# Gated graph layer: the products of a zero matrix between the block sums are taken out

## The chip, the cores and the metric

One core of one Trainium2 chip runs the whole program. A core has five engines that run beside each other and wait for one another by semaphores: TensorE (PE, matmuls; PEld is its loading of the stationary operand), VectorE (DVE), ScalarE (ACT), GpSimd (POOL) and SyncE (SP, which only issues DMAs here). The metric is the device time of one execution in microseconds (us), lower is better; a measured time is the median of several runs. [...]

## The reference, cut to what matters

The program is two graph layers and two expert layers over 3,125 nodes with 256 features and 100,000 edges. The change lies in the third part, the gated graph layer:

```python
def _L1_gnn_ref(x, src, dst, W_w, W_b, U_w, U_b, V_w, V_b, attn_l, attn_r, gamma, beta):
    Wh = x @ W_w + W_b
    Uh = x @ U_w + U_b
    Vh = x @ V_w + V_b
    out_src = Wh * attn_l
    out_dst = Wh * attn_r
    sigma = jax.nn.sigmoid(out_src[src] + out_dst[dst])
    sum_sigma_h = jax.ops.segment_sum(Vh[src] * sigma, dst, num_segments=N)
    sum_sigma = jax.ops.segment_sum(sigma, dst, num_segments=N)
    h = Uh + sum_sigma_h / (sum_sigma + 1e-06)
    mu = jnp.mean(h, axis=-1, keepdims=True)
    var = jnp.mean((h - mu) ** 2, axis=-1, keepdims=True)
    h = (h - mu) / jnp.sqrt(var + 1e-06) * gamma + beta
    h = jax.nn.relu(h)
    return x + h
```

Its result is normalized again and goes through the first linear layer with a GELU and the gate (`gelu(xn @ W1 + b1)`, `@ Wg + bg`) of the last expert layer, which `stage_strips` computes on the way.

## The kernel before, in words

The stages run one after another. `stage_strips` is the gated layer. The nodes lie in 25 blocks of 128 (`NB`), a block in four strips of 32 nodes. A block takes 10 steps (`QC`), so there are 250 steps `g`, with `i = g % 10`. In steps i = 0 to 7 each strip brings 128 edges of its own (tiles of 128 x 1024: four strips of 256 features); in steps 8 and 9 there is one group of 128 mixed edges (128 x 256).

A step passes through the engines like this; the names in quotes are those of the tiles, without the stage's prefix `strips_`:

- POOL (L2461) gathers the rows of the edges' source nodes, one indirect DMA for each strip: 4 in steps 0 to 7, 1 in step 8, 33 for a block (and a single one for all the tenth steps). They land in a ring of 12 slots (`RING`; eight slots are parts of `Wd`, four are `G`). A slot is asked for again once the gate product of its last user is done (`s_use`). The last block has only two strips with edges of their own, so it has 17 gathers.
- DVE makes the two masks (L2475 `ohT`, L2478 `oh`) two steps ahead.
- PE `expand` (L2627) multiplies the destination nodes' rows by `ohT` into `p_b`: four matmuls of 96 x 256, bf16. It runs two steps ahead too.
- DVE `add` (L2494): `tv` = gathered row + `p_b`. ACT (L2568, L2571): two sigmoids of `tv`, into `p_s` and into half of `sv`. DVE (L2504): gathered row x `p_s` into the other half of `sv`.
- PE `sums` (L2639): `sv` is added into the block's 32-node strips of `p_sg`, four f32 matmuls side by side in the array (eight records in the trace).

Between the steps of a block stand the pieces of the three blocks ahead of it (`tail(b, i)`): layer norms on DVE; on PE the transposes of the normalized block (L2661, with step i = 4), the linear layer (L2672) in groups of 6, 6 and 4 products of f32 (12, 12 and 8 records) with steps i = 5, 6 and 7, the gate (L2681, L2686) and the transposes of the hidden rows (L2688 with i = 2, L2693 with i = 4); on ACT the copy `xT` of the transposed block (L2590, i = 4), the GELU (L2599, i = 9). Every engine runs its list strictly in that written order. So ACT cannot start the sigmoids of the step after i = 4 before `xT` is copied, and `xT` needs PE's `sums` of step i = 4 and the transposes behind it.

On PE the list of one step is: `expand(g + 2)`; in the steps i = 1 to 4 four products of the zero tile `nil` (128 x 128 by 128 x 512, bf16) that are added to the block's sum `p_sg`; `sums(g)`; and the tails. The zero products (L2650) wait for nothing but the buffer's one memset (L2553).

Of the kernel before, what the change touches and what calls it, by code (L numbers as in the profile page):

```python
# [15 lines left out]
BF16 = mybir.dt.bfloat16  # L16
# [7 lines left out]
P = 128  # L24
N = 3125
D = 256
# [11 lines left out]
H = 4  # L38
# [40 lines left out]
QC = QR + QM  # L79
QB = -(-N // 32)  # L80
NG4 = NB * QC
RR = 4
RING = 12
QP = 32
# [54 lines left out]
def alloc(nc, ctx, stage=""):  # L139

    def sb(name, shape, dt=F32):
        return ctx.enter_context(nc.sbuf_tensor(stage + name, shape, dt))

    def ps(name, shape, dt=F32):
        return ctx.enter_context(nc.psum_tensor(stage + name, shape, dt))

    sems = []

    def clear():

        if sems:
            nc.clear_and_free_semaphores(sems)  # L152
            for s in sems:
                nc.release_semaphore(nc.alloc_semaphore(s.name + "_back", s.num))

    ctx.callback(clear)

    def sem(name):
        sems.append(nc.alloc_semaphore(stage + name))
        return sems[-1]  # L160

    return sb, ps, sem
# [2146 lines left out]
def stage_strips(nc, C, A):  # L2309


    with ExitStack() as ctx:
        sb, ps, sem = alloc(nc, ctx, "strips_")
        G = [C.Wd[:, k * FC * D:(k + 1) * FC * D].rearrange("p (h d) -> p h d", h=H) for k in range(NE)] + [sb(f"G{k}", [P, H, 2 * D]) for k in range(NE, RING)]
        row = [sb(f"row{k}", [ST, H, P], BF16) for k in range(RR)]; ipt = sb("ipt", [ST, P]); ip = sb("ip", [ST, 1])
        oh = [sb(f"oh{k}", [P, H, QP]) for k in range(4)]; nil = sb("nil", [P, 2 * D], BF16)
        ohT = [sb(f"ohT{k}", [ST, H * P], BF16) for k in range(2)]
        tv = [sb(f"tv{k}", [P, H, D]) for k in range(2)]; wrs = [sb(f"wrs{k}", [ST, H, D], BF16) for k in range(3)]
        sv = [sb(f"sv{k}", [P, H, 2 * D]) for k in range(2)]
# [6 lines left out]
        p_sg = [ps(f"p_sg{k}", [P, 2 * D]) for k in range(2)]; p_h = ps("p_h", [P, F])  # L2326
        s_g = [sem(f"s_g{k}") for k in range(RING)]
        Gs = sb("Gs", [P, 1, 2 * D]); s_gs = sem("s_gs")
        s_row = [sem(f"s_row{k}") for k in range(RR)]; s_ip = sem("s_ip"); s_wr = [sem(f"s_wr{k}") for k in range(3)]; s_oT = sem("s_oT"); s_nil = sem("s_nil"); s_oh = sem("s_oh"); s_b = sem("s_b"); s_t = sem("s_t")
        s_s = sem("s_s"); s_s2 = sem("s_s2"); s_use = sem("s_use"); s_sg = sem("s_sg"); s_tot = sem("s_tot")  # L2330
        s_u = [sem(f"s_u{k}") for k in range(2)]; s_w = sem("s_w"); s_wg = sem("s_wg"); s_l4 = sem("s_l4"); s_lt = sem("s_lt"); s_d = sem("s_d"); s_ur = sem("s_ur"); s_var = sem("s_var"); s_std = sem("s_std")
        s_q = sem("s_q"); s_var2 = sem("s_var2"); s_std2 = sem("s_std2"); s_n = sem("s_n"); s_xn = sem("s_xn"); s_tr = sem("s_tr"); s_hr = sem("s_hr"); s_hd = sem("s_hd"); s_xd = sem("s_xd"); s_Wd = sem("s_Wd")
# [57 lines left out]
        with nc.Block(no_gpsimd_drain=True) as block:  # L2390
# [77 lines left out]
            def _(v):  # L2468
                with when_even(C, v, 1):
                    def masks(g):  # L2470
                        b, i = divmod(g, QC)
                        v.wait_ge(s_row[g % RR], 16 * (g // RR + 1))
                        if g >= 2:
                            v.wait_ge(s_b, g - 1)
                        nc.vector.tensor_scalar(ohT[g % 2][:, :], row[g % RR][:, :, :].rearrange("p j e -> p (j e)"), ip[:, 0:1], None, ALU.is_equal).then_inc(s_oT, 1)  # L2475
                        if g >= 4:
                            v.wait_ge(s_sg, g - 3)
                        nc.vector.tensor_tensor(oh[g % 4][:, :, :], C.iota[:, 0:QP].unsqueeze(1).broadcast_to([P, H, QP]),  # L2478
                                                C.dlq[:, b * H:(b + 1) * H, i:i + 1].broadcast_to([P, H, QP]), ALU.is_equal).then_inc(s_oh, 1)
# [70 lines left out]
                            v.wait_ge(s_l, b + 1)  # L2550
                            nc.vector.tensor_tensor(C.lg[:, b, :], ffn(b)[:, 512:512 + NE], bg[:, :], ALU.add).then_inc(s_lg, 1)

                    nc.vector.memset(nil[:, :], 0.0).then_inc(s_nil, 1)  # L2553
                    masks(0)
                    masks(1)
                    nc.vector.memset(wgp[:, :, :], 0.0).then_inc(s_wg, 1)
# [60 lines left out]
            def _(pe):  # L2617
                with when_even(C, pe, 1):
                    def expand(g):
                        b = g // QC  # L2620
                        pe.wait_ge(s_oT, g + 1)
                        if g % QC == 0:
                            pe.wait_ge(s_wr[b % 3], 48 * (b // 3 + 1))
                        if g >= 1:
                            pe.wait_ge(s_t, g)
                        for j in range(H):
                            t = nc.tensor.matmul(p_b[:, j % wide(g), :], ohT[g % 2][:, j * P:j * P + P], wrs[b % 3][:, j, :],  # L2627
                                                 start=(j < wide(g)), stop=(wide(g) == H or j == H - 1))
                        t.then_inc(s_b, 1)

                    def sums(g):
                        b, i = divmod(g, QC)
                        pe.wait_ge(s_use, g + 1)
                        pe.wait_ge(s_s, g + 1)
                        pe.wait_ge(s_oh, g + 1)
                        if i == 0 and b >= 2:
                            pe.wait_ge(s_tot, 2 * b - 2)
                        for j in range(H):
                            t = nc.tensor.matmul(p_sg[b % 2][j * QP:(j + 1) * QP, :], oh[g % 4][:, j, :], sv[g % 2][:, j % wide(g), :],  # L2639
                                                 start=(i == 0), stop=(i == QC - 1), tile_position=(0, j * QP))  # L2640
                        t.then_inc(s_sg, 1)

                    def group(g):
                        if g + 2 < NG4:
                            expand(g + 2)
                        if g == 1:
                            pe.wait_ge(s_nil, 1)
                        if 1 <= g % QC < 5:
                            for n in range(4):
                                nc.tensor.matmul(p_sg[g // QC % 2][:, :], nil[:, 0:P], nil[:, :], start=False, stop=False)  # L2650
                        sums(g)

                    def tail(b, i):
# [42 lines left out]
                    expand(0)  # L2696
                    expand(1)
                    each_step(group, tail)


# [672 lines left out]
def build(nc, A, out):  # L3373
# [19 lines left out]
    with ExitStack() as ctx:  # L3393
# [46 lines left out]
        with ExitStack() as second:  # L3440
            sb, ps, sem = alloc(nc, second)
            C.ixq = sb("ixq", [P, QN, QR, 2], I32); C.mixed = sb("mixed", [P, NB + 1, 2], I32); C.dlq = sb("dlq", [P, QN, QC])
            stage_experts(nc, C, A)
            ahead.close()
            stage_gated_in(nc, C, A)
            bias.close()
            C.Wd = ctx.enter_context(nc.sbuf_tensor("Wd", [P, NE * FC * D], F32, side="right"))
            stage_strips(nc, C, A)
# [48 lines left out]
```

## Time and profile before

| | us |
|---|---|
| median of 3 runs | 3048.69 (3047.15 to 3051.67) |
| profiled execution: span from its first to its last instruction | 3050.2 |
| share of the span: PE busy | 2502.4 (82%) |
| DVE busy | 2395.6 (79%) |
| POOL busy | 1359.9 (45%) |
| ACT busy | 1169.5 (38%) |
| first gather of `stage_strips` issued, at | 1783.55 |
| last gather issued, at | 2804.42 |
| last matmul of the stage starts, at | 2865.03 |

The page gives no time of the profiled execution other than its span. Times "at" count from the first instruction of the program. The stage with the change lasts from about 1783 to 2866, some 1083 us of the 3050. A busy share is a mean over stages that have different limits, so what bounds this stage has to be read from its own waits. In a row of the timeline the first number is the start, the second how long the instruction or merged group was busy, and brackets hold the engine's idle time before it with the engine that ended it; "issue" stands for time in which it waited for nothing that the profile shows.

### The profile page before, as it was taken

The page shows a single profiled execution, that of the slowest core. Times are in us where ns is not written, and L with a number is a line of the kernel's source. Part 1 is how long each engine was busy: PE and PEld are TensorE (multiplying, and loading weights), DVE is VectorE, ACT ScalarE, POOL GpSimd, SP SyncE. Part 2 cuts the span into 40 slices and gives each one's busy share as a digit, 9 for nine tenths or more (in the row PEclk, how much of TensorE's full clock was granted, in tenths as well). Part 3 has the DMA queues.
Part 4 walks back from the last instruction along what each step waited for, and adds up shares of the span by engine and source line. Part 5 has one row for each costly group of instructions (what it writes and reads, how often), then busy time and mean ns, then how long its engine had stood idle before and what let it go on. Part 6 is the DMA issues. An engine that isn't in the chain of part 4 may idle for free. (4 is left out here: it accounts for less than half of the span.)

```text
span 3050.2 us, 49528 instructions
## 1 busy us (share of the span) xinstructions
PE 2502.4 (82%) x17163; PEld 1226.6 (40%) x17164; DVE 2395.6 (79%) x5109; ACT 1169.5 (38%) x2265; POOL 1359.9 (45%) x1627
## 2 busy tenths in 40 slices
PE   6899869999986999985999756777666777667598
PEld 3555544333353333334666421333333333323365
DVE  6999979999968999979343757777777777777477
ACT  5666750000020000002222434666666666666421
POOL 2888850000000000000650777777777777776055
PEclk8999989999998999995999876888888888888799
DMA  3000010000032000003341577888888888887343
GB/s 123 10 10 10 10 38 15 15 15 15 5 42 40 15 26 18 5 19 107 92 124 43 189 239 240 247 258 259 248 256 259 255 259 256 252 258 241 133 148 106
DMA packets 235579, 373.47 MB, mean 122 GB/s; under 512 B 83273, under 2 KB 165390, under 8 KB 233513
## 3 DMA queue, kind: packets, MB, share of 16 engines
q0 software_dynamic: 75536, 238.14, 25.9%
q1 hardware_dynamic: 156569, 128.66, 14.2%
q10 hardware_dynamic: 3200, 3.21, 0.4%
q8 instruction: 147, 2.41, 0.3%
q14 instruction: 127, 1.04, 0.1%
HBM read 324.84 MB, written 50.04 MB: 123 GB/s over the span
## 5 line engine op out<-in xcount | busy, mean ns | idle before, releaser
L1161 PE MATMUL dense_p_o<-dense_W,feat 128*32 128x512 f32 x7200 | 789.7, 594 | 23.4 <-DVE dense_W L1093 23.4
L1093 DVE SCALAR_TENSOR_TENSOR dense_W<-layer_B,steep,cnt 128x512 f32<-128x512 f32 x1200 | 796.7, 744 | 3.2 <-DVE dense_W L1093 1.8
L2461 POOL DMA_INDIRECT Wd<-tab_d,ixq x544 | 520.7, 957 | 171.2 <-issue 167.5
L1161 PEld LDWEIGHTS dense_p_o<-dense_W,feat 128*32 128x32 f32 x7200 | 261.4, 110 | 520.9 <-issue 399.9
L1572 POOL MEMSET edst<- 128x782 int32 x1 | 0.8, 752 | 936.6 <-POOLq L1210 936.6
L2639 PE MATMUL strips_p_sg<-strips_sv,strips_oh 128*32 128x512 f32 x2000 | 317.7, 713 | 92.7 <-DVE strips_sv L2504 92.7
L2627 PE MATMUL strips_p_b<-strips_wrs,strips_ohT 96*128 96x256 bf16 x1000 | 176.5, 306 | 223.2 <-DVE strips_ohT L2475 204.6
L729 POOL TENSOR_SCALAR mix_L<-mix_back,encode_lowT 128x128 bf16<-128x128 f32 x520 | 320.5, 634 | 55.6 <-PE mix_p_c L889 54.8
L2568 ACT ACTIVATE strips_p_s<-strips_tv 128x1024 f32<-128x1024 f32 (+1 forms) x250 | 225.2, 901 | 163.9 <-DVE strips_sv L2504 149.7
L1117 ACT COPY dense_part<-dense_p_o 128x512 f32<-128x512 f32 x36 | 18.8, 594 | 645.5 <-PE dense_p_o L1161 645.5
L2461 POOL DMA_INDIRECT strips_G<-tab_d,ixq x240 | 229.7, 957 | 73.2 <-issue 71.3
L2494 DVE TENSOR_TENSOR strips_tv<-Wd,strips_p_b 128x1024 f32<-128x1024 f32 (+1 forms) x152 | 175.6, 1155 | 99.8 <-DMA Wd<-tab_d,ixq 61.2
L2627 PEld LDWEIGHTS strips_p_b<-strips_wrs,strips_ohT 96*128 96x128 bf16 x1000 | 94.0, 106 | 360.3 <-DVE strips_ohT L2475 317.2
L2571 ACT ACTIVATE strips_sv<-strips_tv 128x1024 f32<-128x1024 f32 (+1 forms) x250 | 228.6, 914 | 0.1
L2504 DVE TENSOR_TENSOR strips_sv<-Wd,strips_p_s 128x1024 f32<-128x1024 f32 (+1 forms) x152 | 174.7, 1149 | 63.4 <-ACT strips_p_s L2568 63.2
L738 DVE TENSOR_SCALAR mix_R<-encode_ramp,encode_keyT 128x250 bf16<-128x250 uint16 (+2 forms) x784 | 183.1, 299 | 0.0
L746 DVE TENSOR_TENSOR cnt<-cnt,mix_p_c 128x500 f32 x196 | 130.7, 667 | 23.9 <-PE mix_p_c L889 21.6
L889 PE MATMUL mix_p_c<-mix_R,mix_L 128*128 128x250 bf16 (+2 forms) x784 | 128.7, 291 | 14.9 <-DVE cnt L746 12.6
L2650 PE MATMUL strips_p_sg<-strips_nil 128*128 128x512 bf16 x400 | 136.3, 475 | 0.0
L2672 PEld LDWEIGHTS strips_p_h<-strips_xT,strips_w 128*128 128x128 f32 x768 | 104.7, 216 | 65.2 <-issue 65.2
L2639 PEld LDWEIGHTS strips_p_sg<-strips_sv,strips_oh 128*32 128x32 f32 x2000 | 42.1, 115 | 189.4 <-DVE strips_sv L2504 139.4
L2672 PE MATMUL strips_p_h<-strips_xT,strips_w 128*128 128x128 f32 x768 | 118.1, 309 | 0.0
(540 smaller groups left out, 3883.2 us busy)
## 6 DMA issues: line engine op xcount, KB each, us to landing
strips_row<-dlr_d SPq DMA_DIRECT2D x250, 96.0 KB
ew<-in_ew SPq DMA_DIRECT2D x16, 1024.0 KB, 5.4
layer_B<-rise_d SPq DMA_DIRECT2D x12, 1024.0 KB, 4.8
hx_d<-hrow SPq DMA_DIRECT2D x24, 512.0 KB, 2.8
Wd<-tab_d,ixq POOLq DMA_INDIRECT x544
Wd<-in_fWd SPq DMA_DIRECT2D x8, 1024.0 KB, 9.0
tab_d<-feat SPq DMA_DIRECT2D x50, 128.0 KB, 2.5
tab_d<-gated_in_rowg SPq DMA_DIRECT2D x25, 256.0 KB, 2.0
```

What stands on the lines that cost most here:

```text
L729: nc.gpsimd.tensor_scalar(L[g % NL][:, j, :], back[:, :], lowT[:, i, j * CP + p:j * CP + p + 1], None, ALU.is_equal).then_inc(s_Lp, 1)
L738: nc.vector.tensor_scalar(own(g, j), near_keys(j), keyT[:, i, j * CP + p:j * CP + p + 1], None, ALU.is_equal).then_inc(s_oh, 1)
L1093: o = nc.vector.scalar_tensor_tensor(out=out, in0=rise, scalar=C.steep[:, q * H + h:q * H + h + 1], in1=count, op0=ALU.max, op1=ALU.mult)
L1161: m = nc.tensor.matmul(p_o[c % 2][h * MT:(h + 1) * MT, a, 0:n], feat[:, q, h, lo:lo + MT], W[t % 3][:, h, 0:n], start=(q == 0), stop=(q == ...
L2461: gp.indirect_dma_start(out=G[n % RING][:, j, :], out_offset=None, in_=C.tab3[:, :], in_offset=bass.IndirectOffsetOnAxis(ap=index, axis=0) ...
L2494: nc.vector.tensor_tensor(tv[g % 2][:, 0:wide(g), :], rows(g)[:, :, 0:D], p_b[:, 0:wide(g), :], ALU.add).then_inc(s_t, 1)
L2504: nc.vector.tensor_tensor(sv[g % 2][:, 0:wide(g), 0:D], rows(g)[:, :, D:2 * D], p_s[:, 0:wide(g), :], ALU.mult).then_inc(s_use, 1)
L2568: nc.scalar.activation(p_s[:, 0:wide(g), :], tv[g % 2][:, 0:wide(g), :], ACT.Sigmoid).then_inc(s_s2, 1)
L2571: nc.scalar.activation(sv[g % 2][:, 0:wide(g), D:2 * D], tv[g % 2][:, 0:wide(g), :], ACT.Sigmoid).then_inc(s_s, 1)
L2627: t = nc.tensor.matmul(p_b[:, j % wide(g), :], ohT[g % 2][:, j * P:j * P + P], wrs[b % 3][:, j, :], start=(j < wide(g)), stop=(wide(g) == ...
L2639: t = nc.tensor.matmul(p_sg[b % 2][j * QP:(j + 1) * QP, :], oh[g % 4][:, j, :], sv[g % 2][:, j % wide(g), :], start=(i == 0), stop=(i == Q ...
L2672: t = nc.tensor.matmul(ffn(b)[:, q * P:q * P + P], w1[:, kc, q * P:q * P + P], xT[:, kc * P:kc * P + P], start=(kc == 0), stop=(kc == KC - 1))
```

## The change

The four zero products are taken out of the steps i = 1 to 4 of each block, with the tile `nil`, its memset on DVE, its semaphore and PE's one wait for it. They are 4 x 4 x 25 = 400 matmuls and as many weight loads. What they added to the sums was zero.

```diff
-        oh = [sb(f"oh{k}", [P, H, QP]) for k in range(4)]; nil = sb("nil", [P, 2 * D], BF16)
+        oh = [sb(f"oh{k}", [P, H, QP]) for k in range(4)]
...
-                    nc.vector.memset(nil[:, :], 0.0).then_inc(s_nil, 1)
                     masks(0)
                     masks(1)
...
                     def group(g):
                         if g + 2 < NG4:
                             expand(g + 2)
-                        if g == 1:
-                            pe.wait_ge(s_nil, 1)
-                        if 1 <= g % QC < 5:
-                            for n in range(4):
-                                nc.tensor.matmul(p_sg[g // QC % 2][:, :], nil[:, 0:P], nil[:, :], start=False, stop=False)
                         sums(g)
```

No other instruction changes its place on any engine. PE's list at a step i = 4 of a block and at i = 5 behind it, before (`strips_p_b` is `expand`, `strips_nil` the zero tile, `strips_p_sg<-strips_sv` the sums, `strips_p_h` the transposes and the linear layer):

```order
L2627 MATMUL strips_p_b<-strips_wrs,strips_ohT 128x256 x4
L2650 MATMUL strips_p_sg<-strips_nil 128x512 x4
L2639 MATMUL strips_p_sg<-strips_sv,strips_oh 32x512 x4
L2693 MATMUL strips_p_h<-ident,strips_HT 128x128 x4
L2661 MATMUL strips_p_h<-ident,strips_xn 128x128 x2
L2627 MATMUL strips_p_b<-strips_wrs,strips_ohT 128x256 x4
L2639 MATMUL strips_p_sg<-strips_sv,strips_oh 32x512 x4
L2672 MATMUL strips_p_h<-strips_xT,strips_w 128x128 x6
```

and the same place on PE in the changed kernel, where the line numbers are smaller by 1 to 6:

```order
L2626 MATMUL strips_p_b<-strips_wrs,strips_ohT 128x256 x4
L2638 MATMUL strips_p_sg<-strips_sv,strips_oh 32x512 x4
L2687 MATMUL strips_p_h<-ident,strips_HT 128x128 x4
L2655 MATMUL strips_p_h<-ident,strips_xn 128x128 x2
L2626 MATMUL strips_p_b<-strips_wrs,strips_ohT 128x256 x4
L2638 MATMUL strips_p_sg<-strips_sv,strips_oh 32x512 x4
L2666 MATMUL strips_p_h<-strips_xT,strips_w 128x128 x6
```

The row of the zero products is gone and nothing has moved past anything else.

## Rows read from the trace of the kernel before

**Rows 1.** The page: busy time of the engines; POOL and granted clock in 40 slices.

```profile
PE 2502.4 (82%) x17163; PEld 1226.6 (40%) x17164; DVE 2395.6 (79%) x5109; ACT 1169.5 (38%) x2265; POOL 1359.9 (45%) x1627
...
POOL 2888850000000000000650777777777777776055
PEclk8999989999998999995999876888888888888799
```

**Rows 2.** Stretches of the stage: blocks 1 to 22, last block, its tail.

```profile
core 0: us, PE busy (x) PEld busy (x) DVE busy (x) ACT busy (x) POOL busy (x), PEclk, DMA share, GB/s
...
1833.00:2753.60 920.60, 659.62 (x4243) 290.40 (x4246) 683.92 (x1233) 581.42 (x857) 698.37 (x730) 0.85 0.84 254
...
2798.00:2839.00 41.00, 30.94 (x196) 13.97 (x199) 30.68 (x55) 26.48 (x40) 5.70 (x6) 0.83 0.82 265
2839.00:2866.00 27.00, 18.62 (x162) 14.70 (x159) 6.96 (x20) 15.67 (x43) 0.00 (x0) 0.81 0.21 72
```

**Rows 3.** Timeline of POOL: the first gather, two in block 23, the last.

```profile
1783.55 0.98 POOL L2461 DMA_INDIRECT Wd<-tab_d,ixq  x1 [5.66 <-issue]
...
2757.70 0.95 POOL L2461 DMA_INDIRECT Wd<-tab_d,ixq  x1 [0.30 <-issue]
2758.96 0.95 POOL L2461 DMA_INDIRECT Wd<-tab_d,ixq  x1 [0.30 <-issue]
...
2804.42 0.94 POOL L2461 DMA_INDIRECT strips_G<-tab_d,mixed  x1 [0.30 <-issue]
```

**Rows 4.** Waits from 1833 to 2753.6: total us, times, longest us.

```profile
DVE strips_tv L2494 <- DMA Wd<-tab_d,ixq: 34.9, 27, 2.7
DVE strips_tv L2494 <- PE strips_p_b L2627: 26.3, 24, 2.1
DVE strips_tv L2494 <- DMA strips_G<-tab_d,ixq: 20.7, 15, 2.7
...
POOL Wd L2461 <- DVE strips_sv L2504: 3.4, 11, 0.3
```

**Rows 5.** Timeline of DVE: a product in block 22, steps 229, 230, 240, 249.

```profile
2718.02 1.22 DVE L2504 TENSOR_TENSOR strips_sv<-Wd,strips_p_s 128x1024 f32<-128x1024 f32 x1 [0.72 <-ACT strips_p_s L2568]
...
2751.11 0.42 DVE L2494 TENSOR_TENSOR strips_tv<-strips_Gs,strips_p_b 128x256 f32<-128x256 f32 x1 [0.96 <-PE strips_p_b L2627]
...
2753.64 1.22 DVE L2494 TENSOR_TENSOR strips_tv<-Wd,strips_p_b 128x1024 f32<-128x1024 f32 x1 [1.31 <-issue]
...
2798.06 1.22 DVE L2494 TENSOR_TENSOR strips_tv<-Wd,strips_p_b 128x1024 f32<-128x1024 f32 x1 [1.31 <-issue]
...
2836.96 0.42 DVE L2494 TENSOR_TENSOR strips_tv<-strips_Gs,strips_p_b 128x256 f32<-128x256 f32 x1 [0.96 <-issue]
```

**Rows 6.** Timeline of the last block's steps 4 to 6: PE, one DVE product.

```profile
2821.81 1.21 DVE L2504 TENSOR_TENSOR strips_sv<-Wd,strips_p_s 128x1024 f32<-128x1024 f32 x1
...
2822.19 1.29 PE L2650 MATMUL strips_p_sg<-strips_nil 128*128 128x512 bf16 x4
2823.41 1.94 PE L2639 MATMUL strips_p_sg<-strips_sv,strips_oh 128*32 128x512 f32 x8
...
2829.25 1.59 PE L2639 MATMUL strips_p_sg<-strips_sv,strips_oh 128*32 128x512 f32 x8 [2.21 <-DVE strips_sv L2504]
2830.77 2.69 PE L2672 MATMUL strips_p_h<-strips_xT,strips_w 128*128 128x128 f32 x12
...
2833.82 1.06 PE L2639 MATMUL strips_p_sg<-strips_sv,strips_oh 128*32 128x512 f32 x8
2834.82 1.60 PE L2672 MATMUL strips_p_h<-strips_xT,strips_w 128*128 128x128 f32 x12
```

**Rows 7.** What is removed: the zero products' group (page), the memset and first sum.

```profile
L2650 PE MATMUL strips_p_sg<-strips_nil 128*128 128x512 bf16 x400 | 136.3, 475 | 0.0
...
1783.95 0.27 DVE L2553 MEMSET strips_nil<- 128x256 uint32 x1
...
1794.57 1.22 DVE L2494 TENSOR_TENSOR strips_tv<-Wd,strips_p_b 128x1024 f32<-128x1024 f32 x1 [7.63 <-DMA Wd<-tab_d,ixq]
```

More of the change, by code:

```diff
@@ L2328, in stage_strips @@
         Gs = sb("Gs", [P, 1, 2 * D]); s_gs = sem("s_gs")
-        s_row = [sem(f"s_row{k}") for k in range(RR)]; s_ip = sem("s_ip"); s_wr = [sem(f"s_wr{k}") for k in range(3)]; s_oT = sem("s_oT"); s_nil = sem("s_nil"); s_oh = sem("s_oh"); s_b = sem("s_b"); s_t = sem("s_t")
+        s_row = [sem(f"s_row{k}") for k in range(RR)]; s_ip = sem("s_ip"); s_wr = [sem(f"s_wr{k}") for k in range(3)]; s_oT = sem("s_oT"); s_oh = sem("s_oh"); s_b = sem("s_b"); s_t = sem("s_t")
         s_s = sem("s_s"); s_s2 = sem("s_s2"); s_use = sem("s_use"); s_sg = sem("s_sg"); s_tot = sem("s_tot")
```

## The prediction

> **What bounds the kernel now.** I started with the page's busy shares. PE is the busiest engine of the program at 82% [rows 1], which would make every matmul taken out look like a gain. But the change touches one stage only, so I cut that stage into stretches. In the 920.6 us of blocks 1 to 22, PE is busy 659.62 us, DVE 683.92 and ACT 581.42 [rows 2]: none is full. The reader is to see in the same row that POOL has 730 gathers in it, one in 1.26 us. The timeline of POOL says why: two gathers in a row start at 2757.70 and 2758.96, each 0.95 us long with 0.30 us of its own issue before it [rows 3]. That is 1.25 us for a gather however full the other engines are. From 1783.55 to 2804.42 [rows 3] the 810 gathers (24 x 33 + 17 + 1) take 1020.9 us, or 1.26 each. POOL hardly ever stands for a buffer: its waits for DVE's products add up to 3.4 us, the longest 0.3, which is no more than its issue time [rows 4].
>
> The waits confirm it from the other side. DVE's first sum of a step waits for a gather to land 27 + 15 times in that stretch, 34.9 + 20.7 = 55.6 us, 2.5 us for each of the 22 blocks [rows 4]. So the chain of DVE, ACT and PE follows the gathers and catches up with them in most blocks.
>
> How much room lies between the two: the product at 2718.02 ends at 2719.24 and frees the slot of step 220 [rows 5]; twelve slots later that slot is asked for at 2757.70, the first gather of step 233 [rows 3]. The chain could run 38.5 us later before POOL would feel it. But a chain that is late at the end is late by just that amount, ring or no ring, because the last block has half the gathers and is not paced by them: the last gather is issued at 2804.42 [rows 3] and the last sum starts at 2836.96 [rows 5]. What counts is whether the chain keeps up over a block, and how long the last block and its tail take.
>
> The chain's own pace is seen where no gather holds it. In the last block it goes from step 240 at 2798.06 to step 249 at 2836.96, 38.90 us for nine steps; a tenth like the one from 2751.11 to 2753.64 is 2.53, so 41.4 us for a block [rows 5]. Thirty-three gathers at 1.2526 take 41.3 us, and the 22 blocks took 920.6 / 22 = 41.8 each [rows 2]. The two are close. That is the danger in this case: a block is not bound by PE, but a block that gets longer by more than a microsecond or two will be.
>
> **The change, part by part.** *The 400 zero products.* They kept PE busy for 136.3 us [rows 7], 5.5 us a block. In blocks 0 to 23 this is PE time inside a stage that POOL paces, so it is worth nothing as such: the gathers hide it. It can only matter where a zero product runs on past the end of the DVE product that the sums wait for. In step 244 that product ends at 2821.81 + 1.21 = 2823.02 and the sums start at 2823.41, when the zero products are through: 0.39 us late, and behind these sums stand the transposes, ACT's copy and the next sigmoids [rows 6]. In the last block this comes back in full: -0.4 us. In the others it lies behind the gathers: 0. Were the cover gone, it would be -0.4 each, or 24 x -0.4 = -10 us.
>
> *The memset.* DVE loses 0.27 us at 1783.95, and its first sum then waits 7.63 us for the first gather [rows 7]: 0. PE's wait for it never held. The free kilobyte in each partition moves later tiles; no row shows an address to matter, so 0, with nothing to bound it by but the scatter of the runs.
>
> *TensorE's clock.* This is the part with a sign of its own. The granted share in blocks 1 to 22 is 0.85 [rows 2]: PE is at half clock about 30% of the time although the zero products fill its gaps. A row shows what comes before a fall: PE idle 2.21 us for a DVE product, then sums of 1.59 us, where the same sums take 1.06 two steps on [rows 6]. Without the zero products the steps 1 to 4 hold only the expansion and the sums, so PE is idle for most of them, and I expect the half level to spread over these four steps. What it makes of one instruction is in the rows: sums 1.06 to 1.94 us, twelve records of the linear layer 1.60 to 2.69 [rows 6]. In steps 1 to 3 nobody waits for the sums of the same step; the next users come two steps later, so 0.88 us more is hidden. It is not hidden in two places. One is step 4, where the transposes go to ACT; but there the sums are at half clock already in the block shown (1.94), so little is added, and the zero products' delay goes: between -0.4 and, where the sums now run at full, +0.88 - 0.4 = +0.5. The other is steps 5 to 7, where PE has sums and linear layer back to back and is the bound of its steps. In the block shown the first of these groups is slow (1.59 + 2.69 against 1.06 + 1.60, +1.6), the second is fast. If the half level now lasts through the second as well, a block gets 0.88 + 1.09 = 2.0 us longer. That is less than the 2.5 us of waiting for gathers in a mean block [rows 4]. So in blocks 0 to 23 I take 0, with ends of 0 and +2.0 a block. In the last block nothing covers it: between -1.6 (its first group at full) and +2.0; long stretches of work bring the clock back within such a group now, so I take the value near the lower middle, +0.5.
>
> *The tail*, 27 us from 2839 to 2866 at 0.81 [rows 2], starts 17 us after the last zero product at 2822.19 [rows 6]. Its instructions and idle times are the same: 0, ±1.
>
> Sum: -0.4 + 0.5 + 0 = +0.1 on a profiled span of 3050.2. The median of the runs is 3048.69, 1.5 us below that span and inside the scatter of the runs (3047.15 to 3051.67); so 3049 is what I expect to be measured. The likeliest case has its own range of 3045 to 3055: the last block's -2.0 to +2.5, and the scatter.
>
> [...]
>
> **The rivals.** *Slower: the clock makes the chain longer than the gathers.* The place is steps 5 and 6 of a block, the price 2.0 us where the half level reaches the second linear group, and it decides from the point where a block of the chain passes 41.8 us. For it: a free block already takes 41.4 us, so in blocks like that one only 0.4 of the 2.0 is covered, and lateness adds up from block to block. Against it: the mean of 2.5 us of waiting for gathers, and that PE works without a gap from step 4's sums to the transposes, which should lift the clock again before step 5 or soon in it. If half of the blocks pay, 11 x 2.0 + 2 = 24 us: 3073. All of them, with the 0.4 covered: 24 x 1.6 + 2 = 40: 3089.
>
> *Faster: the chain, not POOL, sets the pace, and the zero products' delay in step 4 is on it.* 24 blocks x 0.4 us, and at most the four products' own 1.29 us [rows 6] in each, gives -10 to -31; near the middle, 3029. For it: the closeness of 41.4 to 41.8. Against it: 42 waits for gathers, spread over 22 blocks.
>
> *Faster by all of it: PE is the bound.* 3050.2 - 136.3 = 2914. Only the 82% speaks for it; DVE's waits for PE's `p_b` are 26.3 us in 24 waits [rows 4], and these stand in the steps that have no zero products.
>
> **How the numbers follow.** A measurement of this kernel can tell a change from none at about 0.2%, 6 us. Forecast (no change, 3049): 0.71. Slower by the clock: 0.20. Faster by the delay: 0.08. PE the bound: 0.01. The range has to leave out no more than 0.2: it holds the first case and, of the slower one, the part in which up to a third of the blocks pay (8 x 2.0 + 2 = 18, so to 3067), and on the low side little, since the delay is small: 3042 to 3067. The chances of faster, same and slower are those of the cases: 0.09, 0.71, 0.20.
>
> **What would show it.** In the profile after: POOL's gathers at 1.25 us still, from about 1783.5 to 2804; DVE's waits for landings still there, near 2 us a block; PE's busy time down by less than 136 us in the stage, because what stays runs slower; the granted clock in blocks 1 to 22 down from 0.85 to somewhere between 0.70 and 0.80 (at 0.60 all of steps 1 to 4, four tenths of the time, would have gone from full to half and more); sums at steps 1 to 4 mostly at 1.94 us, at steps 7 to 9 at 1.06. The forecast is wrong if the last gather is issued later than 2810, or if POOL waits for `sv` by more than its own 0.3 us, or if the landings no longer hold DVE: then the chain is the bound and its lateness is the loss.

## The result, and the profile after

| kernel | median, us | range of the runs, us | profiled span, us |
|---|---|---|---|
| before | 3048.57 (10 runs) | 3044.15 to 3057.83 | 3050.2 |
| changed | 3057.15 (10 runs) | 3052.18 to 3061.25 | 3056.2 |

The ratio is 1.0025, with a 95% interval from 1.0016 to 1.0035. The forecast was 3049 us in a range from 3042 to 3067. The time lies in the range, 8 us above the forecast. The prediction took 0.2% (6 us) as the least that can be told from no change; this interval lies on both sides of it, so the loss is clear of zero and hardly more than that. A second measurement, below, gave 1.0012.

The page of the changed kernel, answering to [rows 1] and [rows 7] (busy time, then POOL and the granted clock in 40 slices, then PE's costliest group in this stage):

```profile
span 3056.2 us, 48728 instructions
...
PE 2492.2 (82%) x16763; PEld 1225.9 (40%) x16764; DVE 2393.3 (78%) x5108; ACT 1169.9 (38%) x2265; POOL 1356.0 (44%) x1627
...
POOL 2888850000000000001650767777777777774055
PEclk8999989999998999985999866777777777776799
...
L2638 PE MATMUL strips_p_sg<-strips_sv,strips_oh 128*32 128x512 f32 x2000 | 366.8, 815 | 123.1 <-DVE strips_sv L2504 122.6
```

The zero products' 136.3 us are gone, yet PE is busy only 10.2 us less. The block sums alone take 366.8 us where the same group took 317.7. They run more often at half clock. The granted share has two levels in all 13 profiles, 1.00 (full clock) and 0.50 (half); from 1833 to 2753.6 us it stood at half for 29% of the time before and for 52% in the changed kernel.

The same stretches of the stage as in [rows 2] (blocks 1 to 22, then the last block):

```profile
1833.00:2753.60 920.60, 648.79 (x3875) 286.31 (x3876) 681.09 (x1232) 582.38 (x857) 697.89 (x732) 0.74 0.83 255
```

```profile
2793.00:2835.00 42.00, 31.12 (x176) 13.71 (x176) 30.87 (x55) 26.58 (x40) 5.94 (x7) 0.67 0.83 264
```

The granted clock fell from 0.85 to 0.74, and POOL issued as many gathers in the same time (732 against 730). POOL's first and last gathers, as in [rows 3]:

```profile
1780.83 0.98 POOL L2461 DMA_INDIRECT Wd<-tab_d,ixq  x1 [5.67 <-issue]
```

```profile
2798.57 0.95 POOL L2461 DMA_INDIRECT Wd<-tab_d,ixq  x1 [0.30 <-issue]
2799.82 0.95 POOL L2461 DMA_INDIRECT strips_G<-tab_d,mixed  x1 [0.30 <-issue]
```

The gathers are 1.25 us apart as before, and the 810 of them took 1019.0 us (1020.9 before). DVE's and POOL's waits from 1833 to 2753.6, as in [rows 4]:

```profile
DVE strips_tv L2494 <- PE strips_p_b L2626: 40.4, 19, 3.1
DVE strips_tv L2494 <- DMA Wd<-tab_d,ixq: 10.2, 9, 3.1
DVE strips_tv L2494 <- DMA strips_G<-tab_d,ixq: 9.4, 5, 4.4
...
POOL Wd L2461 <- DVE strips_sv L2504: 5.2, 17, 0.3
```

DVE's waits for landings shrank from 55.6 us to 19.6, that is from 2.5 us a block to 0.9. Its waits for PE grew by 14.1, and its idle time without a visible cause by 16.8 (from 37.9 to 54.7). So the chain is slower, and the cover of the gathers paid for it. The last block has no such cover. DVE's rows from step 240 on, answering to [rows 5], and PE's, answering to [rows 6]:

```profile
2793.20 1.22 DVE L2494 TENSOR_TENSOR strips_tv<-Wd,strips_p_b 128x1024 f32<-128x1024 f32 x1 [1.28 <-issue]
...
2830.01 0.42 DVE L2494 TENSOR_TENSOR strips_tv<-strips_G,strips_p_b 128x256 f32<-128x256 f32 x1 [3.07 <-PE strips_p_b L2626]
...
2833.30 0.42 DVE L2494 TENSOR_TENSOR strips_tv<-strips_Gs,strips_p_b 128x256 f32<-128x256 f32 x1 [1.28 <-issue]
```

```profile
2818.22 1.93 PE L2638 MATMUL strips_p_sg<-strips_sv,strips_oh 128*32 128x512 f32 x8 [0.29 <-DVE strips_sv L2504]
...
2824.27 1.93 PE L2638 MATMUL strips_p_sg<-strips_sv,strips_oh 128*32 128x512 f32 x8 [1.79 <-DVE strips_sv L2504]
2826.13 2.93 PE L2666 MATMUL strips_p_h<-strips_xT,strips_w 128*128 128x128 f32 x12
...
2829.84 1.39 PE L2638 MATMUL strips_p_sg<-strips_sv,strips_oh 128*32 128x512 f32 x8
2831.16 1.60 PE L2666 MATMUL strips_p_h<-strips_xT,strips_w 128*128 128x128 f32 x12
2833.13 1.07 PE L2638 MATMUL strips_p_sg<-strips_sv,strips_oh 128*32 128x512 f32 x8
```

Steps 240 to 249 took 2833.30 - 2793.20 = 40.10 us, 1.2 more than before; 1.0 of it is the wait of step 248 for the expansion, 3.07 us against 2.08. From the first gather to the last product of this stage (`sv`) it is still 1054.2 us against 1055.1. **The stage that was changed lost nothing.** The loss is behind it. From that product to the end of the span, before took 211.6 us and the changed kernel 221.2, although not one instruction differs there. (The stage's start differs by some 7 us between the two profiled executions of the changed kernel, 1780.8 and 1787.4 us, so spans are a poorer guide than such differences.)

That rest consists of the tail, a preparation, and the final stage. The final stage takes 29 tiles. For each POOL gathers `dense_hx`, PE transposes it (`dense_p_t`) and multiplies it by the expert's weights (`dense_p_y`), and POOL scatters `out`. PE at its entrance, first in before, then in the changed kernel (start, length, operation, idle time ahead of it):

```profile
2902.88 1.97 PE L3351 MATMUL dense_p_t<-ident,dense_hx 128*128 128x128 f32 x8 [0.48 <-DMA dense_hx<-hx_d,dense_where]
2905.29 1.10 PE L3351 MATMUL dense_p_t<-ident,dense_hx 128*128 128x128 f32 x8 [0.44 <-DMA dense_hx<-hx_d,dense_where]
2906.32 3.67 PE L3362 MATMUL dense_p_y<-dense_wt,dense_HT 128*64 128x256 f32 x32
```

```profile
2899.82 1.97 PE L3345 MATMUL dense_p_t<-ident,dense_hx 128*128 128x128 f32 x8 [0.27 <-DMA dense_hx<-hx_d,dense_where]
2904.28 1.97 PE L3345 MATMUL dense_p_t<-ident,dense_hx 128*128 128x128 f32 x8 [2.50 <-DMA dense_hx<-hx_d,dense_where]
2906.18 5.07 PE L3356 MATMUL dense_p_y<-dense_wt,dense_HT 128*64 128x256 f32 x32
```

PE waits 2.50 us for the second gather instead of 0.44. The transposes behind it (1.97 against 1.10) and the first products (5.07 against 3.67) then run at half clock (the transposes whole, the products up to 2909.05, where the granted share goes from 0.50 to 1.00). That makes 2.06 + 0.87 + 1.40 = 4.3 us before the first `out` is scattered. What lay beside the gather is seen in DMA traffic cut to a microsecond: "q8 instruction" is an engine's code being fetched, in packets of 16 KB (147 of them make 2.41 MB on the page of before, 16.4 KB each). Before, 2897 to 2898 us, then the changed kernel, 2901 to 2902:

```profile
q8 instruction: 1, 0.02, 5.5%
issues: line engine op xcount, KB each, median us to landing
dense_hx<-hx_d,dense_where POOLq DMA_INDIRECT x1, 4.9
```

```profile
q0 software_dynamic: 62, 0.29, 83.9%
q8 instruction: 1, 0.02, 6.7%
```

In before the packet starts at 2897.1, ahead of the first gather (2897.94), and nothing else moves in that microsecond. In the changed kernel it starts at 2901.0, among 62 packets of the gathers. The second gather, issued at 2896.53, lands after 7.7 us (5.9 before). The profile's page gives the total of that queue: 147 packets before, 144 after. It is PE's code: in blocks 1 to 22 the queue moved 35 packets for 8489 matmuls and weight loads before and 32 for 7751 after, 242 each in both (instructions of PE that only wait are not counted in that). The change takes 400 matmuls and as many weight loads out of PE's list.

How many instructions a packet holds stands in no view; 256 is the author's estimate, and the runs below bear it out. last_only and first_only have 768 instructions of PE fewer than before and three packets fewer (144), 256 to a packet, and their packet starts 0.7 and 0.8 us ahead of the first gather, as in before (0.8). In all_but_last, with 32 fewer, it starts 5.6 us behind that gather, in the changed kernel, with 800 fewer, 5.9. So 768 instructions leave the fetches where they were, and the other 32 of the 800 move them: they fall 32 instructions later in the program. (The total alone would not do as a measure: first_5, with 640 fewer, has 143.)

In the rows at the entrance PE's idle times (0.27 and 2.50 us in the changed kernel) end with a landing of `dense_hx`, not with code. What goes with the packet is seen on POOL's gather.

### The profile page after: what moved, and what is told of

It reads as the page before. It is cut to its first block and busy times, and to the rows that moved or that the text cites. A ratio compares the mean times of both kernels' runs of the same rounds, so it can differ in the third digit from the quotient of the medians.

```text
span 3056.2 us, 48728 instructions
## 1 busy us (share of the span) xinstructions
PE 2492.2 (82%) x16763; PEld 1225.9 (40%) x16764; DVE 2393.3 (78%) x5108; ACT 1169.9 (38%) x2265; POOL 1356.0 (44%) x1627
## 5 line engine op out<-in xcount | busy, mean ns | idle before, releaser
L2638 PE MATMUL strips_p_sg<-strips_sv,strips_oh 128*32 128x512 f32 x2000 | 366.8, 815 | 123.1 <-DVE strips_sv L2504 122.6
L2626 PE MATMUL strips_p_b<-strips_wrs,strips_ohT 96*128 96x256 bf16 x1000 | 201.1, 338 | 202.5 <-DVE strips_ohT L2475 183.8
L729 POOL TENSOR_SCALAR mix_L<-mix_back,encode_lowT 128x128 bf16<-128x128 f32 x520 | 318.9, 630 | 56.5 <-PE mix_p_c L889 55.6
L2626 PEld LDWEIGHTS strips_p_b<-strips_wrs,strips_ohT 96*128 96x128 bf16 x1000 | 105.1, 117 | 373.0 <-DVE strips_ohT L2475 321.2
L2666 PEld LDWEIGHTS strips_p_h<-strips_xT,strips_w 128*128 128x128 f32 x768 | 117.6, 239 | 71.1 <-issue 71.1
L2666 PE MATMUL strips_p_h<-strips_xT,strips_w 128*128 128x128 f32 x768 | 131.8, 334 | 0.0
L2504 DVE TENSOR_TENSOR strips_sv<-strips_G,strips_p_s 128x1024 f32<-128x1024 f32 (+1 forms) x73 | 78.1, 1070 | 47.9 <-ACT strips_p_s L2567 47.9
```

The lines of the kernel that those rows point to most:

```text
L729: nc.gpsimd.tensor_scalar(L[g % NL][:, j, :], back[:, :], lowT[:, i, j * CP + p:j * CP + p + 1], None, ALU.is_equal).then_inc(s_Lp, 1)
L2504: nc.vector.tensor_tensor(sv[g % 2][:, 0:wide(g), 0:D], rows(g)[:, :, D:2 * D], p_s[:, 0:wide(g), :], ALU.mult).then_inc(s_use, 1)
L2666: t = nc.tensor.matmul(ffn(b)[:, q * P:q * P + P], w1[:, kc, q * P:q * P + P], xT[:, kc * P:kc * P + P], start=(kc == 0), stop=(kc == KC - 1))
```

## The experiments

All ratios are to runs of before on the same chip. "Fetches later by", the shift, says by how many instructions the fetches of PE's code fall later in the program than in before: what is missing from PE's list, less whole packets of 256, by the estimate above (400 products are 800 instructions, so 800 - 768 = 32; 192 later is the same as 64 sooner). "2nd gather" is the landing time of the final stage's second `dense_hx` gather. "Rest" is the time from the last `sv` to the end of the span. Both are from the one profiled execution. Medians of different sessions differ by up to 5.6 us for the same kernel, so kernels are compared by the ratio. The last two kernels compute something else (below).

| kernel | zero products kept | fetches later by | median, us | ratio, 95% | 2nd gather, us | rest, us |
|---|---|---|---|---|---|---|
| before | 400 | 0 | 3048.57 | - | 5.9 | 211.6 |
| before_again | 400 | 0 | 3053.54 | 0.9999 (0.9990 to 1.0008) | 6.3 | 211.7 |
| last_only | 16 | 0 | 3052.35 | 0.9992 (0.9983 to 1.0000) | 6.6 | 213.3 |
| first_only | 16 | 0 | 3053.04 | 1.0002 (0.9994 to 1.0011) | 6.3 | 213.2 |
| first_3 | 48 | 192 | 3054.83 | 1.0009 (0.9999 to 1.0020) | 6.3 | 212.9 |
| first_5 | 80 | 128 | 3052.23 | 1.0001 (0.9992 to 1.0010) | 6.0 | 211.1 |
| first_7 | 112 | 64 | 3057.59 | 1.0012 (1.0003 to 1.0021) | 6.2 | 214.5 |
| changed | 0 | 32 | 3057.15 | 1.0025 (1.0016 to 1.0035) | 7.7 | 221.2 |
| after_again | 0 | 32 | 3059.26 | 1.0012 (1.0002 to 1.0023) | 8.3 | 217.7 |
| all_but_last | 384 | 32 | 3056.36 | 1.0010 (0.9998 to 1.0022) | 7.4 | 220.5 |
| all_but_13th | 384 | 32 | 3058.20 | 1.0013 (1.0005 to 1.0022) | 7.6 | 217.4 |
| few_before | 400 | 0 | 3039.67 | 0.9958 (0.9943 to 0.9973) | 5.9 | 216.5 |
| few_after | 0 | 32 | 3046.36 | 0.9972 (0.9961 to 0.9984) | 6.4 | 214.4 |

**The two kernels again.** after_again and before_again are the changed kernel and before, unedited.

> The changed kernel a second time, unchanged. Its first profile has the strips stage no longer than before (first gather to last gate product 1054.2 us against 1055.1), while the stretch from there to the end is 9.6 us longer (221.2 against 211.6), most of it in the final expert stage. Theory A (the chain of DVE, ACT and PE in the strips stage has lost its slack and is late in most executions, just not in the profiled one): this profile shows the stage some 5 to 10 us longer, with the final stage as before. Theory B (the loss is at the end of the strips stage and at the entrance of the final stage, where TensorE comes in at half clock): stage again the same, the end again 5 to 10 us longer. Theory C (the final stage's waits for gathered rows differ from execution to execution and the profiled one was unlucky): end within 3 us of before. All three: ratio to before 1.002 to 1.003.

> The kernel before a second time, unchanged: what the profile of one more execution says of the scatter. Expected by all theories: ratio 1.000 with an interval of 0.1% on either side. Stage from first gather to last gate product 1055 us within 2, the stretch from there to the end 212 us within 3. If that last stretch moves by 5 us or more between two executions of one kernel, the 9.6 us seen between the two first profiles are no evidence for theory B.

The loss came again, at half its first size: 1.0012, below the 1.002 to 1.003 expected. before_again stands at 0.9999. So the true loss is some 0.1 to 0.3%. The changed stage took 1054.3 us, as in the first profile, and the rest of the span is again longer than before's, 217.7 us. before_again's rest is 211.7, as expected; its stage took 1052.7, a little outside the 1055 ± 2 expected. So the stage varies by some 2 us from one execution of a kernel to the next, and the rest of before by 0.1 in these two.

**Zero products in the last block alone, and in all but the last.**

```diff
-                        if 1 <= g % QC < 5:
+                        if 1 <= g % QC < 5 and g // QC == NB - 1:   # last_only
+                        if 1 <= g % QC < 5 and g // QC < NB - 1:    # all_but_last
```

> The zero products only in the last of the 25 blocks (16 of 400). Theory A (loss in the paced blocks 0 to 23): as slow as the changed kernel, ratio 1.002 to 1.003. Theory B (loss in the last block and at the entrance of the final stage): back to the time of before, ratio 1.000. Granted clock of the stage near 0.74 by both.

> The zero products in all blocks but the last (384 of 400). Theory A: time of before, ratio 1.000. Theory B: as slow as the changed kernel, 1.002 to 1.003. Granted clock of blocks 1 to 22 at 0.85 by both.

last_only did as well as before, and all_but_last came out at 1.0010, which is no certain loss by itself. Taken alone that looks as if the last block's zero products were worth 3 us. But all_but_last's stage, first gather to last `sv`, took 1053.1 us, between the 1055.1 and 1052.7 of the two profiles of before. Its rest took 220.5. So the last block had not lost the time, and the same split had two readings: which block keeps them, or how long PE's list is.

**The same two shifts with the last block the other way round.** Both readings are set against each other.

```diff
-                        if 1 <= g % QC < 5:
+                        if 1 <= g % QC < 5 and g // QC == 0:    # first_only
+                        if 1 <= g % QC < 5 and g // QC != 12:   # all_but_13th
```

> The zero products only in block 0 (16 of 400). The traces so far fall into two kinds: where the last block had its zero products and the list of PE is shorter by 0 or 768 instructions (before, last_only), a code fetch of 16 KB lies just before the first gather of the final stage and the second gather lands 5.9 to 6.6 us after its issue; where the last block had none and the list is shorter by 32 or 800 (all_but_last, the changed kernel), the fetch lies in the middle of that second gather, which takes 7.4 to 8.3, and the stretch behind the strips stage is 6 to 10 us longer. [...] Theory D (code fetch): what counts is the number of instructions before the final stage, modulo 256; this kernel has 768 fewer, so the fetch is back before the first gather, the stretch behind the strips stage is 211 to 214 us, ratio 0.999. Theory B (last block's zero products): this kernel has none there, so as slow as the changed one: stretch 217 to 221, ratio 1.001 to 1.003.

> The zero products in all blocks but the 13th (384 of 400); PE's list is shorter by 32, as in all_but_last. Theory D: fetch in the middle of the second gather of the final stage, stretch behind the strips stage 217 to 221 us, ratio 1.001 to 1.002. Theory B: the last block is as before, so stretch 211 to 214, ratio 1.000.

first_only has no zero product in the last block and is even with before (1.0002). all_but_13th has them there and loses (1.0013). Both rests are what theory D, the place of the code fetch, had named beforehand (213.2 and 217.4). The last block's zero products are not the cause. The first also shows what the removal itself does, with the fetches left in place. Its clock over blocks 1 to 22 is the changed kernel's, and so are DVE's waits for gathers, 13.5 + 9.1 = 22.6 us:

```profile
1833.00:2753.60 920.60, 644.80 (x3868) 283.92 (x3866) 682.23 (x1229) 580.51 (x854) 698.29 (x730) 0.74 0.84 254
```

```profile
DVE strips_tv L2494 <- DMA Wd<-tab_d,ixq: 13.5, 15, 2.6
DVE strips_tv L2494 <- DMA strips_G<-tab_d,ixq: 9.1, 6, 2.6
```

**Other shifts.** The condition is `g // QC < 3`, `< 5` and `< 7`.

```diff
-                        if 1 <= g % QC < 5:
+                        if 1 <= g % QC < 5 and g // QC < 5:   # first_5; 3 and 7 likewise
```

> The zero products stand in blocks 0 to 2 alone (48 of 400), so TensorE's list is 704 instructions shorter than before's: 64 more than 256 times a whole number below it. Theory D (place of TensorE's code fetches in the final stage): the 16 KB fetch that began at 2897.1 us in before, just ahead of the first dense_hx gather, comes 64 instructions sooner in the program, in the tail, some 5 to 10 us ahead of that gather, and the one at 2916.0 us comes to about 2908 to 2912, after the first four gathers were issued. The second gather lands 5 to 6.5 us after its issue (7.4 to 8.3 where the fetch fell on it), and the time from the last sv on is 209 to 214 us. Ratio to before 0.997 to 1.001. Rival (the removal itself costs, the more zero products are gone): 352 of 400 are gone, so 1.002 or more, as in the changed kernel. Rival C (any shift of the code away from before's own place costs): from the last sv on 217 us or more.

> Zero products in blocks 0 to 4 alone (80 of 400): TensorE's list is 640 instructions shorter, 128 off before's place in a fetch of 256. Theory D: the fetches that stood at 2897.1 and 2916.0 us in before come half a fetch sooner, that is one in the tail near 2885 and one near 2905 to 2909, behind the first four gathers of the stage; if it comes before these have landed it holds the third or fourth and not the second. From the last sv on 209 to 216 us; ratio 0.997 to 1.002. Rival (the removal itself): 1.002 or more. Rival C (any other place costs): 217 us or more from the last sv on.

> Zero products in blocks 0 to 6 alone (112 of 400): TensorE's list is 576 instructions shorter, which puts the fetch 64 instructions later than in before and 32 later than in the changed kernel (there 2901.0 us, in the middle of the second gather, 7.7 us from issue to landing). Theory D: it begins 3 to 6 us later than in the changed kernel against the first gather, so while the third or fourth gather is under way; the second lands after 5 to 6.5 us, and a part of the loss stays, since the third or fourth is held: from the last sv on 211 to 219 us, ratio 0.999 to 1.002. Rival (the removal itself): 1.002 or more. If the second gather is held as long as in the changed kernel, the reading of the fetch's place by instruction count is wrong.

The fetches came in the expected order: in first_3 at 2913.7 (2908 to 2912 were expected), 13.6 us behind the first gather, in first_5 9.8 behind it and in first_7 8.1. In the changed kernel it is 5.9, so first_7's is later by 2.2 and not by the 3 to 6 expected; it falls while the third gather is under way, but that one is hardly held (6.4 us to landing, 6.1 in before). In none was the second gather held, and none had a rest of 217 us or more, so a place other than before's does not cost by itself (rival C). first_5, without 320 of the 400 zero products, is even with before, which goes against "the more are gone, the slower".

first_7 is the one that theory D does not explain. Its second and third gather landed in time. Yet PE stayed at half clock into the first products (granted share 0.50 up to 2916.32 us; in first_5 up to 2905.45), and the measured ratio is 1.0012. first_5, then first_7:

```profile
2906.43 1.10 PE L3351 MATMUL dense_p_t<-ident,dense_hx 128*128 128x128 f32 x8 [0.73 <-DMA dense_hx<-hx_d,dense_where]
2907.45 3.67 PE L3362 MATMUL dense_p_y<-dense_wt,dense_HT 128*64 128x256 f32 x32
```

```profile
2910.06 1.97 PE L3351 MATMUL dense_p_t<-ident,dense_hx 128*128 128x128 f32 x8 [0.77 <-DMA dense_hx<-hx_d,dense_where]
2911.96 5.81 PE L3362 MATMUL dense_p_y<-dense_wt,dense_HT 128*64 128x256 f32 x32
```

The idle times are alike (0.73 and 0.77). The half-clock stretch lasted 17.1 us against 10.2. That is worth 0.87 + 2.14 = 3.0 us, nearly all by which first_7's rest (214.5) exceeds first_5's (211.1). Why the clock came back in one and not in the other, these runs don't say.

**What the zero products are worth where no gather covers them.** Both kernels gather two instead of four times in a wide step from the third round of the ring on, so half of the rows that these steps read are left from earlier steps. That part of the computation is left out.

```diff
-        return min(H, QB - b * H) if i < QR else 1 if i == QR else 0
+        return min(H if slot(g) < 2 * RING else 2, QB - b * H) if i < QR else 1 if i == QR else 0
```

> The kernel before with two gathers instead of four in each wide step from the third ring round on (the other strips read rows left in the ring from earlier steps, so the sums are not the reference's). That takes the gathers' pace away: 17 for a block instead of 33, so that the chain of DVE, ACT and PE alone sets the time of blocks 3 to 24. It tests the step of the prediction that calls the clock's cost hidden. Expected: a block of 39.8 us where step 5 runs at full clock and 41.4 at half, so 40.3 in the mean, the stage about 1.2 us a block or 25 us shorter, ratio 0.992. If POOL was not what paced the stage: ratio 1.000.

> The changed kernel with the same halved gathers (sums not the reference's). The difference to few_before is what the zero products are worth where nothing covers the clock. If the cover of my forecast is real: 1 to 1.5 us a block slower than few_before, since steps 5 to 7 lose more at half clock than step 4 gains from the missing products; 25 to 35 us in all, ratio to before 1.000 to 1.002. If the chain is not longer by the clock: equal to few_before but for the end of the program, 5 to 8 us.

few_before took 3039.67 us, ratio 0.9958 (0.9943 to 0.9973), and few_after 3046.36, 0.9972 (0.9961 to 0.9984). Neither came where it was expected (0.992, and 1.000 to 1.002). POOL now waits for DVE by up to 5.4 us at a time, 265.6 us from 1900 to 2700 in few_before. Before, the longest such wait was 0.3. The last line is the clock in few_after over the same stretch:

```profile
POOL Wd L2461 <- DVE strips_sv L2504: 265.6, 100, 5.4
```

```profile
1900.00:2700.00 800.00, 568.04 (x3498) 257.19 (x3502) 599.68 (x1089) 519.72 (x771) 329.00 (x347) 0.76 0.55 162
```

From the start of block 4 to that of block 23, a mean block of the free chain takes 40.94 us with the zero products and 41.12 without. That is 0.2 us a block; the whole stages, 1036.6 and 1041.6 us, differ by 5.0. The mean hides two patterns. From block 3 on, 6 of few_before's 21 blocks took 39.8 to 40.2 us and the other 15 took 41.3 to 41.5. In few_after 17 of the 21 took 40.9 to 41.3. With gathers in full the same mean was 41.48 and 41.57 (41.73 in before_again). So the gathers do set the pace, but by some half a microsecond a block only. These runs take away the issue of the gathers and their traffic together (162 GB/s in few_after, 254 before); that it is the issue is read from POOL's rows, 1.25 us apart, and not shown by a run of its own.

## Why the prediction was right, and where it failed

**The gathers set the pace of blocks 0 to 23, so PE's 136.3 us are worth nothing there: shown.** They stayed at 1.25 us, 1019.0 us in all. The stage kept its length in the changed kernel (1054.2 and 1054.3 against 1055.1 and 1052.7) and in last_only and first_only (1054.7 and 1054.2). Where half of the gathers were gone, the ratio fell to 0.9958, some 13 us, so they were what bound it. "PE is the bound" (2914 us) is refuted.

**The clock falls to between 0.70 and 0.80, with the sums of steps 1 to 4 at half: right, but for step 1.** It was 0.74. A group of sums counts as half here when it took over 1.5 us (1.06 at full, 1.94 at half). The sums of steps 2, 3 and 4 ran so in all 25 blocks (in 32, 8 and 60% of them before), those of step 1 in 40% only (16% before). Those of steps 7 to 9 hardly ever did. Step 5's sums ran at half in 64% of the blocks (32% before).

**The cover of 2.5 us a block: right in kind, thinner than the text made it.** "DVE's waits for landings near 2 us a block" came out at 0.9. The stage was 0.9 us a block from being bound by its chain, so the first rival was near. It didn't decide, since the free chain is only 0.2 us a block slower (few_after), not the 2.0 at which the rival priced every block. The 0.2 is a net figure: the zero products' own delay, 0.4 us in step 4, goes with them, and no run parts it from what the clock costs. The chain's block was also read too long: 41.4 us from the last block, 40.9 in few_before. (The 1.2526 us that the prediction gives for a gather stands in none of its rows; they give 0.95 + 0.30 = 1.25, and 33 of them make 41.3 either way.)

**The last block: +0.1 forecast, +1.2 measured in the profile** (inside the -2.0 to +2.5 given). Its second linear group ran fast, 1.60 us, as chosen. The first ran at 2.93 (2.69 before), and step 248 waited 3.07 us for the expansion (2.08 before). last_only keeps the zero products there and first_only doesn't; their stages differ by 0.5 us and their ratios' intervals overlap, so a microsecond here can't be told in the times.

**The step that failed: the sum ends with "The tail [...] Its instructions and idle times are the same: 0, ±1".** The tail itself came as forecast, 27.5 us against 27.0. But behind it the sum counted nothing, without a reason. The rest measured +9.6 us in the first profile (211.6 to 221.2) and +6.0 in the second (211.7 to 217.7), while the stage before it kept its length. The final stage lost the remainder: 4.1 us up to its first `out` (37.6 against 33.5), and 4.7 or 2.3 between the first and the last `out` (139.3 and 136.4 against 134.6 and 134.1). One row of the later part, the changed kernel in the thirteenth interval between two scatters:

```profile
2973.07 1.21 PE L3345 MATMUL dense_p_t<-ident,dense_hx 128*128 128x128 f32 x8 [2.19 <-DMA dense_hx<-hx_d,dense_where]
```

The gather it waited for was issued at 2966.84 and landed after 6.2 us; its neighbours, with no fetch on them, took 5.2. The products behind it took 5.19 us against 3.67; the granted share was 0.50 from 2973.91 to 2977.32. The DMA traffic from 2967.2 to 2967.6 holds it and a code packet:

```profile
q0 software_dynamic: 32, 0.06, 40.2%
q8 instruction: 1, 0.02, 24.9%
issues: line engine op xcount, KB each, median us to landing
dense_hx<-hx_d,dense_where POOLq DMA_INDIRECT x1, 6.2
```

"Same instructions, same time" left out that their place in the list had moved by 32. The forecast's three rivals had no such case. That the time fell into the range is luck in this part: the range was open upward for the clock, and the microseconds came from elsewhere.

How far this cause is shown. Of the eleven profiles of kernels that gather in full, the four with fetches 32 instructions later have the second gather at 7.4 to 8.3 us and the rest at 217.4 to 221.2. The seven others have 5.9 to 6.6 and 211.1 to 214.5. Neither the number nor the place of the zero products orders them so.

The later gathers of the final stage say more. In all 13 profiles together the trace has the landing of 243 gathers from the fifth to the 27th tile. For 156 of them no packet of PE's code was in flight between issue and landing, and none took more than 5.7 us. For 87 there was one, and 21 of these took 5.8 to 7.0 us. Where the packet began 2.5 to 4.7 us behind the issue, 15 of 21 took over 6.0. So a slow gather always had a code packet beside it, but a packet does not always make one slow. before, before_again and first_5 have no such slow gather among these, last_only has two, first_only three and first_3 one; their rests are 211.6, 211.7 and 211.1 us against 213.3, 213.2 and 212.9.

Two kernels speak against the simple form of this cause. few_after has PE's list of the changed kernel, and its packet falls into the second gather too (at 2890.3 us, the gather issued at 2885.92), but that gather landed after 6.4 us, and the first products ran at full clock (granted share 1.00 from 2891.05 on):

```profile
2892.35 1.09 PE L3345 MATMUL dense_p_t<-ident,dense_hx 128*128 128x128 f32 x8 [1.12 <-DMA dense_hx<-hx_d,dense_where]
2893.37 3.67 PE L3356 MATMUL dense_p_y<-dense_wt,dense_HT 128*64 128x256 f32 x32
```

Its rest is 214.4 us. few_before has its fetches where before has them, and a rest of 216.5. Their sums differ, so the rows that they gather here may differ as well; no run tells whether that is the reason.

Not shown, then: that the packet itself holds the gather up (it coincides, and moves as counted, but no run took it away), and what holds first_7's clock. That clock alone brought first_7's first `out` 17.9 us behind its first gather, with no gather late; the four had 18.0 to 18.7, the six others 14.6 to 15.3. So how much of the four's loss at the entrance is the gather and how much the clock is open. The ratios alone don't prove the cause either: the four stand at 1.0010 to 1.0025, and first_7 (1.0012) and first_3 (1.0009) reach into that. first_3 and all_but_last (1.0010) could each be taken for no change.

No version that computes the reference's result beat before. last_only, at 0.9992 (0.9983 to 1.0000), comes nearest. Where the fetches stay in place, as in last_only and first_only (1.0002), taking out 384 of the 400 zero products costs nothing and gains nothing.

## What to carry to other kernels

Read a stage's pace from the engine that never waits: here 136 us of PE work and a tenth of the clock came and went behind gathers of 1.25 us. Then ask how thin the cover is, in microseconds a block after the change and not before it. And when a change of a long list of instructions moves the time by 0.1 to 0.3% and the profile puts it in a stage that wasn't touched, compare where the code fetches fall before explaining it by the stage that was edited; a second version with nearly the same edit and another count of instructions helps to tell the two apart.

## What the runs showed of the hardware

- In the final stage, from the fifth tile on, no gather of 128 rows without a packet of PE's code (16 KB, 0.9 to 1.6 us) in flight took over 5.7 us to land (156 gathers); with one, 21 of 87 took 5.8 to 7.0. At the stage's entrance, where gathers overlap, the second took 7.4 to 8.3 us with the packet in four profiles (mean 7.75), but 6.4 in few_after, and 5.9 to 6.6 without it in seven.
- In the changed kernel a gather later by 2 us went with 4.3 us lost at the stage's entrance: PE's transposes and the first of the products behind it ran at half clock (granted share 0.50 up to 2909.05 us; 1.97 and 5.07 us against 1.10 and 3.67).
- The granted clock fell from 0.85 to 0.74 in 920.6 us, and the stage didn't get longer (1054.2 us against 1055.1). Two levels are all that the 13 profiles show, 1.00 and 0.50; a group of sums took 1.06 us at the one and 1.94 at the other.
